# First norm, mix and norm of a four-layer kernel placed batch by batch ahead of the wider attention, with one semaphore for each load and the token differences on GpSimd

## What is computed

```python
def mix(x):                                  # L0_ffn, used twice
    x_prev = x shifted by one token, zero first
    xr = mu_r * x + (1 - mu_r) * x_prev
    xk = mu_k * x + (1 - mu_k) * x_prev
    r = sigmoid(xr @ W_r.T)
    return r * (square(relu(xk @ W_k.T)) @ W_v.T)

def wide_attention(h):                       # L0_attn: 16 heads of 64, 512 keys
    scores = q @ k.T + rel_emb[bucket(j - i)]
    return (softmax(scores) @ v) @ wo
```

## Time and profile before

| | us |
|---|---|
| three runs: median | 1231.98 |
| lowest and highest | 1229.59, 1234.54 |
| the profiled execution, its own time | 1233.94 |
| its span in the profile | 1232.1 |
| busy: PE, DVE, ACT, POOL | 1146.5, 906.7, 888.2, 607.1 |

### The profile page before, as it was taken

The page is one execution under the profiler, slowest core; times in us unless marked ns, Lnnn a source line. Parts: engine busy times, 40 slices in busy tenths (PEclk is TensorE's granted clock), DMA queues, the critical chain, the costliest instruction groups (busy, mean ns, idle before and its releaser), DMA issues.

```text
span 1232.1 us, 39942 instructions
## 1 busy us (share of the span) xinstructions
PE 1146.5 (93%) x15750; PEld 694.5 (56%) x15750; DVE 906.7 (74%) x2423; ACT 888.2 (72%) x2392; POOL 607.1 (49%) x396
## 2 busy tenths in 40 slices
PE   4899999999999988799999999989998999999997
PEld 1345655555555553376666666555455566666664
DVE  2498878887878875787777777757677677777773
ACT  4676656666656657688878888867878679778874
POOL 0266655655646652465555554442534446554640
PEclk9999999999999999899999999999999999999999
DMA  5622222222322222311111211010111112111110
GB/s 159 248 58 80 56 66 67 63 71 54 80 55 60 74 54 71 107 32 32 40 40 23 44 40 31 19 31 18 39 23 27 36 31 49 41 31 28 40 40 18
DMA packets 35641, 66.97 MB, mean 54 GB/s; under 512 B 6736, under 2 KB 8208, under 8 KB 35456
## 3 DMA queue, kind: packets, MB, share of 16 engines
q1 hardware_dynamic: 35456, 64.43, 19.9%
HBM read 15.32 MB, written 1.11 MB: 13 GB/s over the span
## 4 chain that ended last, share of the span: by engine, by line
PE 78%; ACT 6%; issue 5%; DVE 5%; DMA 3%; SPq 2%; POOL 1%; DVEq 0%; ACTq 0%; POOLq 0%
PE ps L483 11%; PE ps L462 9%; PE ps L1392 6%; PE ps L1355 5%; PE ps L1322 5%; PE ps L1294 5%; PE ps L1273 4%; PE ps L1263 4%; PE ps L1362 4%; PE ps L1334 3%; PE ps L1264 3%; PE ps L1398 3%; DMA arena<-arena 2%; PE ps L491 2%; PE ps L448 2%
## 5 line engine op out<-in xcount | busy, mean ns | idle before, releaser
L415 POOL TENSOR_TENSOR arena<-arena 128x1024 f32<-128x1024 f32 x128 | 241.2, 1893 | 178.0 <-DVE arena L657 177.9
L568 ACT ACTIVATE arena<-arena 128x512 f32<-128x512 f32 x256 | 182.5, 714 | 138.4 <-DVE arena L643 138.3
L1221 POOL TENSOR_TENSOR arena<-arena 128x1024 f32<-128x1024 f32 x64 | 121.4, 1896 | 227.2 <-DVE arena L1761 227.2
L1590 ACT ACTIVATE arena<-arena 128x128 f32<-128x128 f32 x512 | 198.2, 390 | 27.9 <-DVE arena L1753 27.3
L643 DVE CUSTOM_DVE_ANT_0 arena<-ps,arena 128x512 f32<-128x512 f32 x256 | 164.5, 688 | 48.5 <-PE ps L462 45.8
L1753 DVE CUSTOM_DVE_ANT_0 arena<-ps,near,arena 128x128 f32<-128x128 f32 x512 | 144.7, 347 | 40.0 <-PE ps L1322 40.0
L483 PEld LDWEIGHTS ps<-arena 32*64 32x64 f32 x8192 | 120.8, 130 | 74.0 <-issue 47.6
L653 DVE STREAM_TRANSPOSE arena<-arena 128x1024 f32<-128x1024 f32 x128 | 156.7, 1232 | 2.3 <-POOL arena L415 2.0
L483 PE MATMUL ps<-arena 32*64 32x128 f32 x8192 | 139.3, 274 | 18.8 <-issue 14.8
L1228 POOL TENSOR_TENSOR arena<-arena 128x1024 f32<-128x1024 f32 x64 | 151.0, 2360 | 0.0
L462 PE MATMUL ps<-arena 64*128 64x512 f32 x512 | 144.7, 648 | 2.5 <-DVE arena L643 0.8
(11 more groups left out here) (175 smaller groups left out, 2105.2 us busy)
## 6 DMA issues: line engine op xcount, KB each, us to landing
arena<-arena SPq DMA_DIRECT2D x191, 128.0 KB, 2.4
arena<-arena SPq DMA_DIRECT2D x64, 192.0 KB, 2.6
arena<-rel_rows SPq DMA_DIRECT2D x16, 448.0 KB, 9.0
arena<-arena SPq DMA_DIRECT2D x64, 64.0 KB, 2.1
arena<-y SPq DMA_DIRECT2D x32, 128.0 KB, 2.3
arena<-arena SPq DMA_DIRECT2D x15, 127.8 KB, 2.4
arena<-in_wqkv SPq DMA_DIRECT2D x2, 768.0 KB, 5.1
x<-in_x SPq DMA_DIRECT2D x4, 256.0 KB, 5.2
```

The costliest lines, as they stand in the source:

```text
L415: nc.gpsimd.tensor_tensor(e, e, scale, ALU.mult).then_inc(self.normed, 1)
L568: nc.scalar.activation(self.e[:, r % 3, i, :], self.neg[:, i, :], ACT.Exp, bias=self.nmax[:, i:i + 1], scale=-1.0, accum_out=self.sums[:, ...
L1590: nc.scalar.activation(self.e[:, s, h, :], self.neg[:, h, :], ACT.Exp, bias=self.nmax[:, h:h + 1], scale=-1.0, accum_out=self.sums[:, s, h ...
```

## The change

`LayerNorm` and `ChannelMix` go, and one class, `MixStage`, now serves both places. `Between` is its second use; its first, `Ahead`, places the first norm, the first mix and the second norm batch by batch, in an order of its own for each engine, with the bias rows made between. The last three batches of the second norm come behind the first projections of T5, whose first score waits for all of them. The order of the bank pairs changes with it.

- The constants, the vectors and the small weights each have a semaphore, and x of batch 0 is loaded second. No instruction of PE or ACT waits for DVE's setup before T5.
- The blend is written y_prev + mu * (y - y_prev). The difference is taken once per batch on POOL (`difference`), in place of two scaled copies on ACT; this holds in both uses.
- The first mix takes Exp, add one, Ln and Exp in place of Sigmoid, and squares the key on DVE, as the second did. With that three table loads of ACT go.
- The bias is loaded back for two pairs of heads before T5, and for the others behind the spreads of the first six units. The weights `wo` and the table `rope` are loaded behind the first bias.

```diff
+class MixStage:
...
+    def difference(self, pool, b):
+        k, nc = self.k, self.k.nc
+        pool.wait_ge(*self.first.is_ready(b))
+        if b >= 2:
+            pool.wait_ge(self.mixed, 2 * (self.n0 + b - 2) + 2)
+        nc.gpsimd.tensor_tensor(self.diff[:, b % 2, :], k.y[:, b, 1:PADT], k.y[:, b, 0:T], ALU.subtract).then_inc(self.differed, 1)
+    def blend_in(self, dve, b):
+        k, nc = self.k, self.k.nc
+        dve.wait_ge(self.differed, self.n0 + b + 1)
+        for j in range(2):
+            if b >= 2:
+                dve.wait_ge(self.projected, 2 * (self.n0 + b - 2) + j + 1)
+            nc.vector.scalar_tensor_tensor(out=self.blend[:, b % 2, j, :], in0=self.diff[:, b % 2, :], scalar=k.vcol(C_MUR + j),
+                                           in1=k.y[:, b, 0:T], op0=ALU.mult, op1=ALU.add).then_inc(self.mixed, 1)
...
+    def pool(self, pool):
+        self.difference(pool, 0)
+        self.difference(pool, 1)
+        self.add_one(pool, 0)
+        self.difference(pool, 2)
+        self.add_one(pool, 1)
+        self.difference(pool, 3)
+        self.add_one(pool, 2)
+        self.add_one(pool, 3)
+class Ahead(MixStage):
...
+        first.free = [(x(0), (k.consts_loaded, 16)), (x(1),), (x(2), first.is_ready(0)), (x(3), first.is_ready(1))]
+        second.free = [(self.is_done(0), first.is_ready(3)), (self.is_done(1), second.is_ready(0)), (self.is_done(3),), (self.is_done(3), second.is_ready(1))]
...
+    def pe(self, pe):
+        self.first.centre(pe, 0)
+        self.first.centre(pe, 1)
+        self.first.vary(pe, 0)
+        self.tables.make_rows(pe)
+        self.first.vary(pe, 1)
+        self.first.centre(pe, 2)
+        self.first.centre(pe, 3)
+        self.project(pe, 0)
+        self.first.vary(pe, 2)
+        self.value(pe, 0)
+        self.first.vary(pe, 3)
+        self.project(pe, 1)
+        self.value(pe, 1)
+        self.second.centre(pe, 0)
+        self.project(pe, 2)
+        self.second.vary(pe, 0)
+        self.value(pe, 2)
+        self.project(pe, 3)
+        self.second.centre(pe, 1)
+        self.value(pe, 3)
+    def act(self, act):
+        self.first.square(act, 0)
+        self.first.square(act, 1)
+        self.first.invert(act, 0)
+        self.tables.copy_rows(act)
+        self.first.invert(act, 1)
+        self.first.square(act, 2)
+        self.first.square(act, 3)
+        self.gate(act, 0)
+        self.relu(act, 0)
+        self.first.invert(act, 2)
+        self.open(act, 0)
+        self.first.invert(act, 3)
+        self.gate(act, 1)
+        self.relu(act, 1)
+        self.second.square(act, 0)
+        self.open(act, 1)
+        self.gate(act, 2)
+        self.relu(act, 2)
+        self.second.invert(act, 0)
+        self.open(act, 2)
+        self.gate(act, 3)
+        self.relu(act, 3)
+        self.second.square(act, 1)
+        self.open(act, 3)
+    def dve(self, dve):
+        self.first.scale(dve, 0)
+        self.first.scale(dve, 1)
+        self.blend_in(dve, 0)
+        self.blend_in(dve, 1)
+        self.square_key(dve, 0)
+        self.first.scale(dve, 2)
+        self.add_value(dve, 0)
+        self.first.scale(dve, 3)
+        self.square_key(dve, 1)
+        self.blend_in(dve, 2)
+        self.add_value(dve, 1)
+        self.blend_in(dve, 3)
+        self.square_key(dve, 2)
+        self.second.scale(dve, 0)
+        self.add_value(dve, 2)
+        self.square_key(dve, 3)
+        self.add_value(dve, 3)
...
-class Between:
...
-    def shift(self, act, b):
-        k, nc = self.k, self.k.nc
-        act.wait_ge(self.norm3.ready, b + 1)
-        for j in range(2):
-            if b >= 2:
-                act.wait_ge(self.mixed, 2 * (b - 2) + j + 1)
-            nc.scalar.activation(self.then[:, b % 2, j, :], k.y[:, b, 0:T], ACT.Copy, scale=k.vcol(C_OMR + j)).then_inc(self.shifted, 1)
...
 class T5Tables:
...
     def sp(self, sp):
         k, d = self.k, self.k.dram
-        sp.dma_start(self.onehot, d["onehot"]).then_inc(self.rel_loaded, 16)
-        sp.dma_start(self.rel, d["rel"]).then_inc(self.rel_loaded, 16)
         sp.dma_start(self.wq, d["wq"]).then_inc(self.w_loaded, 16)
         sp.wait_ge(self.rows_copied, 1)
         sp.dma_start(d["rel_rows"], self.rows).then_inc(self.rows_stored, 16)
         sp.wait_ge(self.rows_stored, 16)
-        rows = d["rel_rows"]
-        for h in range(H5):
+        self.load_bias(sp, 0)
+        self.load_bias(sp, 1)
+        sp.dma_start(self.wo, d["wo"]).then_inc(self.wo_loaded, 16)
+        sp.dma_start(k.rope[:, :, :, :], d["rope"]).then_inc(k.rope_loaded, 16)
+    def load_bias(self, sp, pair):
+        rows = self.k.dram["rel_rows"]
+        if pair >= 1:
+            sp.wait_ge(self.bias_loaded, 32 * pair)
+        for h in range(2 * pair, 2 * pair + 2):
             shifted = bass.AP(tensor=rows.tensor, offset=h * DELTAS, ap=[[1, P], [1, BW]])
-            sp.dma_start(self.bias_all[:, h, :], shifted).then_inc(self.first_loaded if h < 2 else self.bias_loaded, 16)
-    def pe(self, pe):
+            sp.dma_start(self.bias_all[:, h, :], shifted).then_inc(self.bias_loaded, 16)
...
 class T5Attention:
                 sp.dma_start(v[0:s, j, :], v[P - s:P, 0, :]).then_inc(self.v_spread, 16)
+            if u + 2 < PAIRS:
+                self.tables.load_bias(sp, u + 2)
...
-        pe.wait_ge(*self.ready(B - 1))
-        pe.wait_ge(self.tables.w_loaded, 64)
+        pe.wait_ge(self.tables.w_loaded, 48)
         def q_proj(u):
             cols = slice(u % PAIRS * P, (u % PAIRS + 1) * P)
+            if u == 0:
+                pe.wait_ge(*self.ahead.is_ready(0))
+                pe.wait_ge(*self.ahead.is_done(2))
...
+            if u == -2:
+                self.ahead.second.centre(pe, 2)
+                self.ahead.second.vary(pe, 1)
+                self.ahead.second.centre(pe, 3)
+                self.ahead.second.vary(pe, 2)
+                self.ahead.second.vary(pe, 3)
+                pe.wait_ge(*self.ahead.is_ready(B - 1))
...
-            if u + 2 < self.UNITS:
+            if u == -2:
+                copy_q(0)
+                self.ahead.second.square(act, 2)
+                self.ahead.second.invert(act, 1)
+                copy_k(0)
+                self.ahead.second.square(act, 3)
+                copy_v(0)
+                self.ahead.second.invert(act, 2)
+                self.ahead.second.invert(act, 3)
+            elif u + 2 < self.UNITS:
...
+        for b in range(1, B):
+            self.ahead.second.scale(dve, b)
         def add_bias(r, i):
-            if u == 1 and r % 2 == 0 and i == 0:
-                dve.wait_ge(self.tables.bias_loaded, 16 * (H5 - 2))
+            if u < PAIRS and r % 2 == 0 and i == 0:
+                dve.wait_ge(self.tables.bias_loaded, 32 * (u + 1))
...
             def _(sp):
-                sp.dma_start(k.consts[:, :], dram["consts"]).then_inc(k.loaded, 16)
-                sp.dma_start(k.vec[:, 0:NVEC], dram["vec"]).then_inc(k.loaded, 16)
-                for b in range(B):
+                sp.dma_start(k.consts[:, :], dram["consts"]).then_inc(k.consts_loaded, 16)
+                sp.dma_start(k.x[:, 0, :], dram["x"][:, 0, :]).then_inc(x_loaded[0], 16)
+                sp.dma_start(k.vec[:, 0:NVEC], dram["vec"]).then_inc(k.vec_loaded, 16)
+                sp.dma_start(k.x[:, 1, :], dram["x"][:, 1, :]).then_inc(x_loaded[1], 16)
+                tables.load_first(sp)
+                sp.dma_start(k.small_w[:, :, :], dram["small_w"]).then_inc(k.small_loaded, 16)
+                for b in range(2, B):
                     sp.dma_start(k.x[:, b, :], dram["x"][:, b, :]).then_inc(x_loaded[b], 16)
-                sp.dma_start(k.small_w[:, :, :], dram["small_w"]).then_inc(k.loaded, 16)
-                for s in plan:
-                    if hasattr(s, "sp"):
-                        s.sp(sp)
+                tables.sp(sp)
+                t5.sp(sp)
+                local.sp(sp)
```

537 lines of the change are left out of this document (199 added, 338 removed).

## The result

| | before | changed |
|---|---|---|
| median of 20 runs each, us | 1231.88 | 1236.13 |
| lowest and highest | 1228.36, 1238.63 | 1229.19, 1242.48 |
| ratio of changed to before | | 1.0034, 95% interval 1.0021 to 1.0047 |
| the profiled execution, its own time | 1233.94 | 1240.86 |
| its span | 1232.1 | 1239.1 |

The changed kernel is slower by 4.3 us. I had forecast 3.0 us faster and a range up to 1233.5; the time lies outside it.

The account below looks back on a forecast made before the run. PE, busy 93% of the span, bounds the kernel outside a 42.5 us start of short dependent steps. Terms -3.5 + 1.0 - 0.5 = -3.0 take 1233.94 to 1230.9, as a median 1229.0 us; range 1223.5 to 1233.5.

Parts of the forecast that it names:

- First matmul: Start of the kernel: with x of batch 0 loaded second, the first matmul at 5.5 us, 6.8 sooner.
- Start, -3.5: Load to first score: first score at 51.3 us against 54.78, half of the earlier first matmul's 6.8 given back.
- the forecast stretch at half rate: First mix, about 33 us: after 3.2 us of PE idleness, value 2 takes 1.7 us and project 3 2.6.
- First scores, +1.0: Start of T5: half rate after 2.9 us of PE idleness, first bias 2.1 us after its score, third 1.7 late.
- Between, -0.5: Second mix: copies' gain shrinks to 0.1 us; a third of the 1.7 from a clock that may stay up.
- the rival of exclusion: DVE and POOL exclude one another: three waits of 1.1 us in the start, +3.3, 1232.3, no gain; chance 0.07.
- The bias loads, 0: T5's first units: loads issued behind the spreads, some 20 us ahead of need, cost nothing.
- T5, 0 with -4 and +4: T5's units: same instructions, shifted pauses; 0 us, with -4 or +4 for one long unit less or more.
- the list of what would prove me wrong: First score before 49 or after 54; DVE standing still as long as POOL's instruction; T5 longer by over 4 us.
- my one slower rival, half rate through the start: Start: about 13 two-pass matmuls on the path cost 0.86 us more each, +11, so +8, 1240; chance 0.06.
- My -3.0: Whole kernel: the sum of the terms, -3.5 + 1.0 - 0.5 us, against the time before.

Follow-up runs that it names:

- experiment 5: Changed kernel with each pair of bias loads issued ahead of its unit's spreads instead of behind them: 1231.53 us, ratio 1.0004 to the kernel before.
- experiment 7: Changed kernel with all bias loads ahead of T5 and two unneeded matmuls before the first scores: 1225.12 us, ratio 0.9949; again, side by side, 1230.18, 0.9987.
- experiment 2: Kernel before with the bias loads of six pairs moved behind the spreads of units 0 to 5: 1237.45 us, ratio 1.0060.
- experiment 4: Changed kernel with the second mix's scaled copies on ACT again instead of differences on POOL: 1235.14 us, ratio 1.0042 to the kernel before.
- early start: Kernel before with only the change's first loads and separate semaphores, stages kept whole: 1226.11 us, ratio 0.9962; again 1222.71, 0.9929.
- experiment 1: Changed kernel with all bias loads ahead of T5, as before the change: 1231.61 us, ratio 1.0002 to the kernel before; side by side again 1231.35, 0.9995.

## Why the prediction was wrong

**First matmul, right.** Forecast 5.5, measured 4.85; in all kernels with x as second load 4.45 to 5.42.

**Start, -3.5: right in size, -2.9; the steps depend on the execution.** The last update of x was to end at 41.55 and ended at 40.56. I had put half rate behind PE's 3.2 us of idleness; in this execution it idled 2.95 us and stayed at full rate. The half rate came in the second norm, where I had none. Busy time by stretch of the changed kernel:
```profile
34.10:37.50 3.40, 2.85 (x8) 1.03 (x6) 2.08 (x3) 1.79 (x3) 1.63 (x1) 1.00 0.00 0
...
45.00:51.80 6.80, 4.51 (x6) 1.62 (x6) 1.32 (x2) 3.43 (x6) 0.00 (x0) 0.75 0.27 72
```
From the last update to the first score it took 11.35, where I had 9.75. The eight other traces with this start do show the forecast stretch at half rate, between 32 and 41 us, behind the same 2.95 us of idleness: in the second execution of the changed kernel from 33.19 to 36.61, and there the last update ended at 41.06. So that step was right for most executions; what I had not counted is half rate in the second norm, which seven of the nine show. In the two without it, those of experiments 5 and 7, 9.90 and 9.80 passed from the last update to the first score, as in my sum.

**First scores, +1.0.** The first bias came 2.23 after its score, forecast 2.1. The whole way to unit 2 grew by 2.9 in this execution, but with the bias loads ahead only by 0.4, at half rate all the same, and by 0.2 in the second execution of the changed kernel: the term was 0.2 to 0.4. The rest is a second stretch at half rate, in unit 1. Busy time by stretch of the changed kernel:
```profile
65.00:72.50 7.50, 7.22 (x14) 3.43 (x15) 7.01 (x18) 5.53 (x14) 6.86 (x4) 0.54 0.59 171
```
Only this execution and that of experiment 5 have it (28.1 and 29.2); three others with late bias loads, the second of the changed kernel and those of experiments 2 and 4, don't, so it can't be put down to the loads alone, and what brings it stays open.

**Between, -0.5: the size fits, the reason doesn't.** DVE's first and last scaling are 42.99 apart before and 42.11 after. But 0.68 of these 0.88 lie ahead of the second scaling, which no difference touches (463.16 to 468.64 before, 470.77 to 475.57 after), and the early start without the differences has that too (453.18 to 457.98). It was a matter of how T5 ended. The mix itself gave 0.1 to 0.2: of the copies' 1.3 only 0.1 was to be left, and so it was. My -0.5 was a third of the gain from a clock that stays up, and it didn't: PE idled 2.17 before value 2, which took 1.79 at 491.91. A difference on POOL took 1.04 here, as I had taken from the square (in the first mix two of four, beside DVE, took 1.48 and 1.54):
```profile
482.51 1.04 POOL L185 TENSOR_TENSOR arena<-y 128x512 f32<-128x512 f32 x1
...
483.56 1.92 POOL L217 TENSOR_SCALAR arena<-arena 128x512 f32<-128x512 f32 x1
...
489.00 2.36 POOL L217 TENSOR_SCALAR arena<-arena 128x512 f32<-128x512 f32 x1
...
489.50 1.75 DVE L193 SCALAR_TENSOR_TENSOR arena<-arena,vec,y 128x512 f32<-128x512 f32 x2
```
The last two rows also settle the rival of exclusion: the pair of blends runs for 1.75 beside an `add_one` of 2.36, each 0.3 to 0.4 longer than alone, and neither stands still. The rule in the Trainium skill ("SBUF — State Buffer", "SBUF: two separate sides") would have stopped the blends until 491.36; the trace disagrees, as in the earlier trace rows.

**The bias loads, 0: the step that failed.** "I cost them at nothing. What is queued behind a load's wait on SP is the next spread, which PE needs 20 us later". That cover was there: no load came late for DVE. The sixteen loads even landed sooner than the earlier trace rows:
```profile
DMA to landing us min/median/max: 3.6/4.5/5.3
```
DVE's waits that the profile puts down to `rel_rows` in units 2, 3 and 5, 0.7 to 0.8 each, are not waits for loads: the pair that unit 2 needs was issued at 52.06, and no load took more than 5.3. At the first of these places (89.06, 0.78) DVE waited 0.63 for the scores before the change, and here too the scores came just ahead. The step that failed is the "nothing": I looked only at who waits for the loads, and not at what else needs the DMA engines while they run. PE's instructions do, and in T5 PE runs through 256 narrow matmuls in 12 us and a long list with them. The pairs are 0.9 MB each, in unit 2 where there had been 5 GB/s. Price: 3.3 us (0.0027, side by side) to 3.9 us (1.0034 against 1.0002, on two occasions), and 0.6% when put into the kernel before. That late packets of queue 8 are the link is read from the traces (89.09 instead of 87.25 in unit 2, 1.25 later against PE's work in unit 4, and all 138 pauses ending just behind such a packet). No run changed the timing of these packets alone: experiment 5, which should have, left the one of unit 4 as late as before. Why the kernel before suffers more (6 us) than the changed one is open as well.

**T5, 0 with -4 and +4.** I had named the mechanism's sign in the list of what would prove me wrong ("longer by more than 4 us, which would be the bias loads or the pauses") but gave it no rival and no chance; my one slower rival, half rate through the start, didn't come. From unit 8 on, T5 took 289.8 to 302.2 in fourteen executions, whatever the edit, so 4 us to either side were rather few for one execution.

**The whole.** With the bias loads ahead, the first score comes 2.6 and 2.1 sooner than before (52.23, 52.65), the way to unit 2 takes 0.4 and 0.2 more, and the stretch between nothing less (43.07 in experiment 1). That leaves some 2 us; the spans say 1.8 and 1.2 less (1230.3 and 1230.9 against 1232.1), and the ratios, 1.0002 and 0.9995, reach down to -1.5 and -2.5 us. My -3.0 would have been too much even without the bias loads, but inside the range.

## What to carry to other kernels

- Traffic that no engine is seen waiting for is not free: before moving loads into a stretch where TensorE runs at 93%, look at what the DMA share is there and at the instruction queue's packets, and keep bulk loads in a stretch that waits anyway (the start of the kernel before held them, with a DMA share of 0.58 from first matmul to first score, at no cost that could be seen).
- When several edits arrive together, ask each for its own gain. Here a dozen lines of semaphores and load order give 0.4 to 0.7%, the new order of the first mix gives some 3.7 us of it back, the spread loads cost 3.3 to 3.9 us, and the differences do nothing that could be told. The best version is the kernel before with early start, with the differences or without: 0.9917 and 0.9929 on one occasion, 0.9962 without them on another.
- A 95% interval covers the scatter of one occasion. Ratios of one kernel on two occasions, on two chips each, differed by 0.33% and 0.38% here; what is to be told apart at this size has to run side by side.
- Nor does one profile speak for the median. The profiled execution can be the fastest or the slowest of its kernel, and what a stretch of it gains can be lost in the next one: compare a stretch in two executions at least.

## What was not expected of the hardware

- Bulk data on the DMA engines holds up TensorE's instruction loads. With 0.85 MB in 3.4 us on them (80%), a packet of 16 KB came 1.8 us later, and TensorE's pauses in the narrow matmuls grew from none to 0.61 and from 1.41 to 2.76 us. Each of 138 pauses ended 1.2 to 1.6 us behind such a packet.
- These pauses come in the same units in all fourteen executions: unit 4 takes 13.5 to 17.9 us and unit 8 14.0 to 19.3 where most take 11.8. With two more matmuls ahead of T5, in three executions, unit 7 takes 13.6 as well.
- The clock after short idle times isn't settled by their length: after 2.95 us at the same place it stayed at 1.00 in one execution and fell to 0.50 within 1.4 us in eight others; after 2.07 it fell 1.15 us behind the first score, after 2.08 in another kernel it stayed at 1.00.
- The first matmuls run at the lower clock although the view reads 1.00 there: the trace has no clock record before 10.95 us (19.73 in experiment 4), and the view counts that as 1.00. In all fourteen traces a pass of 512 columns takes 1.06 us or more up to the first record and 0.59 to 0.70 behind it. The four passes of the bias rows, at nearly the same time in the changed kernel and in experiment 4:
```profile
10.87 1.90 PE L420 MATMUL ps<-arena 32*16 32x512 f32 x4
```
```profile
10.89 3.59 PE L443 MATMUL ps<-arena 32*16 32x512 f32 x4
```
